# SyncE's queue re-ordered, and the split queries' operand loads of the steps requested by ScalarE

## What is computed

```
x   = x + tanh(g_xattn) * attention(layernorm(x), ctx)        # 16 heads of 32, 120 keys
x   = x + tanh(g_ffn)   * int8_linear(layernorm(x))           # rows quantised to -127..127

attention(x, y):  q = x@Wq + bq ; k = y@Wk + bk ; v = y@Wv + bv
                  weights = softmax(q k^T / sqrt(32)) ; out = (weights v) @ Wo + bo
```

## Time and profile before

| | us |
|---|---|
| median of 3 runs | 819.43 (815.38 to 822.44) |
| profiled execution | 818.51 |
| its span, first to last instruction | 816.4 |

### The profile page before, as it was taken

How to read it: one execution, slowest core, us unless ns; L and a number is a source line. 1 busy time by engine, 2 the same in 40 slices (tenths; PEclk the granted TensorE clock), 3 DMA queues, 4 the chain that set the end, 5 groups by cost and what they waited for, 6 DMA issues and landing times.

```text
span 816.4 us, 16283 instructions
## 1 busy us (share of the span) xinstructions
PE 781.1 (96%) x5890; PEld 533.9 (65%) x5890; DVE 587.0 (72%) x879; ACT 604.4 (74%) x844; POOL 527.9 (65%) x524
## 2 busy tenths in 40 slices
PE   9886889999999999999999999999999999999996
PEld 6654556766677676667666676676766677666563
DVE  5964757787686868867686877868688676766567
ACT  5764557868777786877779687777868777796785
POOL 4826328476684947668494756849476685845587
PEclk9989899999999999999999999999999999999999
DMA  8999796878879688897977889697798868775612
GB/s 307 324 256 222 211 262 180 235 230 247 257 195 269 203 241 250 209 273 197 270 222 219 244 231 270 182 266 218 219 268 240 228 177 246 197 186 169 186 66 103
DMA packets 119518, 183.20 MB, mean 224 GB/s; under 512 B 37648, under 2 KB 47248, under 8 KB 117392
## 3 DMA queue, kind: packets, MB, share of 16 engines
q1 hardware_dynamic: 118720, 181.32, 78.3%
q10 hardware_dynamic: 720, 0.86, 0.3%
HBM read 123.91 MB, written 58.22 MB: 223 GB/s over the span
## 4 chain that ended last, share of the span: by engine, by line
PE 80%; DVE 6%; issue 5%; DMA 4%; POOL 2%; ACT 2%; SPq 1%; DVEq 0%; ACTq 0%; POOLq 0%
PE bank_b L443 26%; PE bank_a L443 16%; PE scores L498 7%; PE sum_ps L525 7%; PE scores L517 7%; PE pv_ps L529 6%; PE bank_a L573 4%; DMA q_rows<-q_parts 3%; DVE row_max L1221 2%; PE bank_b L573 2%; PE scores L443 1%; PE bank_a L548 1%; PE sum_ps L506 1%; PE pv_ps L773 1%; DMA k_rows<-o_lo 1%
## 5 line engine op out<-in xcount | busy, mean ns | idle before, releaser
L1232 DVE TENSOR_TENSOR q_parts<-q_sb,q_parts 128x512 fp32r<-128x512 f32 x60 | 64.0, 1066 | 121.5 <-ACT q_parts L857 121.5
L1577 POOL TENSOR_TENSOR o_lo<-on,o_hi 128x512 fp32r<-128x512 f32 x48 | 64.6, 1346 | 131.8 <-ACT o_hi L906 131.8
L1221 DVE TENSOR_REDUCE row_max<-scores 128x16 f32<-128x1920 f32 x64 | 137.7, 2152 | 10.9 <-PE scores L498 10.8
L888 ACT ACTIVATE probs<-scores 120x2048 f32<-120x2048 f32 x64 | 120.1, 1877 | 27.4 <-PE scores L517 27.3
L1533 POOL TENSOR_TENSOR xt<-xt,rstd_b 128x512 f32<-128x512 f32 x60 | 97.3, 1652 | 3.1 <-ACT rstd_b L1155 1.6
L1585 POOL TENSOR_TENSOR x<-x,gbias_r 128x512 f32<-128x512 f32 x64 | 82.9, 1296 | 23.2 <-ACT cen L912 22.1
L498 PEld LDWEIGHTS scores<-k_sb,q_sb 32*128 32x128 f32 x1984 | 61.0, 186 | 52.0 <-issue 41.1
L1573 POOL TENSOR_TENSOR x<-x,gbo_r 128x512 f32<-128x512 f32 x64 | 93.7, 1476 | 0.1
L906 ACT ACTIVATE o_hi<-on 128x512 fp32r<-128x512 f32 x48 | 30.3, 632 | 84.7 <-DVE on L1245 84.7
L517 PE MATMUL scores<-q_stack,k_stack 128*120 128x512 f32 x256 | 74.0, 411 | 17.3 <-DVE row_max L1221 12.5
L443 PE MATMUL bank_b<-xt_hi,wq_hi 128*128 128x512 f32 x188 | 77.4, 412 | 1.3 <-DVE xt_lo L1211 1.2
(11 more groups left out here) (235 smaller groups left out, 1931.8 us busy)
## 6 DMA issues: line engine op xcount, KB each, us to landing
q_stack<-q_rows SPq DMA_DIRECT2D x192, 256.0 KB, 4.5
q_rows<-q_parts SPq DMA_DIRECT2D x61, 512.0 KB, 4.1
xt<-in_x_t SPq DMA_DIRECT2D x16, 1024.0 KB, 8.1
x<-in_x SPq DMA_DIRECT2D x64, 256.0 KB, 3.3
out_x<-x SPq DMA_DIRECT2D x61, 256.0 KB, 5.0
x_in<-in_x SPq DMA_DIRECT2D x60, 256.0 KB, 5.1
k_stack<-k_rows SPq DMA_DIRECT2D x96, 120.0 KB, 3.9
k_rows<-k_parts SPq DMA_DIRECT2D x28, 240.0 KB, 4.0
```

What stands on the lines that cost most here:

```text
L888: act.activation(probs[0:KEYS], scores[0:KEYS], ACT.Exp, scale=SCALE).then_inc(p_ready, 1)
L1221: dve.tensor_reduce(row_max[:].rearrange("p (t r) j -> p r t j", r=ROWG)[:, :, :, j], scores[:, :, 0:QT * KEYS].rearrange("p r (t k) -> p ...
```

## The change

On SyncE:
- `stack_q` is left only three times, ahead of the steps: groups 0, 1 and 2 of batch 0. `stack_q(0, 0)` moves ahead of `store_q(0, 1)`.
- The five loads of `rest_landed` are spread over the issue order between `store_k(0, 3)` and `load_x(3, 0)`; they and a wait for x_stats stood ahead of `load_ctx(1)`.
- Within a step, `load_x(f, 2)` moves to slot 0 behind `store_q(b, 0)` (in step 0: behind `store_q(1, 1)` in slot 1), and `stack_k(b, 0)` moves behind `store_q(b, 1)` and `load_x(f, 3)`.

On ScalarE: `stack_q` is a function of its own, with the same three DMAs and the same two waits, called behind `split_high(b, j)`. Each slot calls it once (slot 0 of step 0 doesn't): `stack_q(i, 2)`, `stack_q(i, 3)`, `stack_q(b, 0)`, `stack_q(b, 1)` in slots 0 to 3; in `last_step` twice. These are 61 calls, 183 DMAs. In slot 3 `high_x(n, 3)` moves ahead of `copy_max`.

The diff, with the moves inside SyncE's list cut to their result:

```diff
@@ SyncE, ahead of the steps
             load_xt(1)
-            sp.wait_ge(x_stats, nth(0, QT, 3))
-            load(rest_landed, u_sb[:].bitcast(I32), rows(wq8))
-            load(rest_landed, gbo_r[:], bo.partition_broadcast(P))
-            load(rest_landed, gws_r[:], w_scale.partition_broadcast(P))
-            load(rest_landed, gbias_r[:], w_bias.partition_broadcast(P))
-            load(rest_landed, ident_b[:], consts_bf16)
             load_ctx(1)
...
             stack_k(0, 0)
+            stack_q(0, 0)
             store_q(0, 1)
-            stack_q(0, 0)
             store_k(0, 2)
             store_k(0, 3)
+            load(rest_landed, u_sb[:].bitcast(I32), rows(wq8))
             stack_q(0, 1)
...
             load_x(2, 2)
+            load_x(2, 3)
+            load(rest_landed, gbo_r[:], bo.partition_broadcast(P))
             stack_q(0, 2)
-            load_x(2, 3)
             store_q(1, 0)
+            load(rest_landed, gws_r[:], w_scale.partition_broadcast(P))
+            load(rest_landed, gbias_r[:], w_bias.partition_broadcast(P))
+            load(rest_landed, ident_b[:], consts_bf16)
             load_x(3, 0)
@@ SyncE, step(i): slots 0 and 1 (slots 2 and 3 lose stack_q(b, 0), stack_q(b, 1); store_q(b, 2) goes ahead of load_x(f + 1, 0))
-                if i > 0:
-                    stack_q(i, 2)
                 if is_batch(e):
                     store(e, 0)
                 if i > 0 and is_batch(b):
                     store_q(b, 0)
+                if i > 0 and is_batch(f):
+                    load_x(f, 2)
                 if i > 0:
                     load_residual(i, 0)
 
-                stack_q(i, 3)
-                if is_batch(f):
-                    load_x(f, 2)
-                if is_batch(b):
-                    stack_k(b, 0)
                 if is_batch(e):
                     store(e, 1)
                 if is_batch(b):
                     store_q(b, 1)
+                if i == 0:
+                    load_x(f, 2)
                 if is_batch(f):
                     load_x(f, 3)
+                if is_batch(b):
+                    stack_k(b, 0)
@@ ScalarE
+            def stack_q(n, j):
+                act.wait_ge(q_stored[j], stores_of(n, j))
+                act.wait_ge(s_done, nth(n, DT, j) - 2)
+                for block, part in enumerate((0, 1, 0)):
+                    load(q_stacked[j % 2], q_stack[j % 2][STRIPS[block]].bitcast(F32),
+                         q_rows[j, part].rearrange("(r d) s -> d r s", d=DH))
@@ ScalarE, step(i), the four slots, and last_step
                     split_high(b, 0)
+                if i > 0:
+                    stack_q(i, 2)
                 log_sums(i, 0)
...
                     split_high(b, 1)
+                stack_q(i, 3)
                 log_sums(i, 1)
...
                     split_high(b, 2)
+                    stack_q(b, 0)
                 log_sums(i, 2)
...
                     split_high(b, 3)
+                    stack_q(b, 1)
...
                     high_x(n, 2)
+                    high_x(n, 3)
                 if is_batch(b):
                     copy_max(b, sum_ps)
                 high_o(i, 3)
-                if is_batch(n):
-                    high_x(n, 3)
...
                 exponentials(i, 0)
+                stack_q(i, 2)
...
                 exponentials(i, 1)
+                stack_q(i, 3)
```

More of the change, by code:

```diff
@@ L385, in step @@
                     store_q(b, 1)
+                if i == 0:
+                    load_x(f, 2)
                 if is_batch(f):
                     load_x(f, 3)
+                if is_batch(b):
+                    stack_k(b, 0)
                 if i > 0:
                     load_residual(i, 1)
-                if is_batch(b):
-                    stack_q(b, 0)
                 if is_batch(k_of(i)):
@@ L396, in step @@
                     store(e, 2)
+                if is_batch(b):
+                    store_q(b, 2)
                 if is_batch(f + 1):
                     load_x(f + 1, 0)
[L399 to L403, removed]
                 if is_batch(k_of(i)):
```

## The result

| | before | after | ratio (95% interval) |
|---|---|---|---|
| median | 817.4 us, 4 runs (814.67 to 822.44) | 806.68 us, 4 runs (804.38 to 809.15) | 0.9869 (0.9832 to 0.9907) |
| timed once more, beside e7, e8 and e10 (e9) | 818.43 us, 14 runs | 805.93 us, 6 runs (805.03 to 811.2) | 0.986 (0.983 to 0.989) |
| profiled execution, its span | 818.51, 816.4 | 809.15, 807.0 | |

The kernel is 1.3% faster, 10.7 us, and the forecast of 807 is met. Most of the terms that were summed to it are not. To see that, I took the start of every `scores_by_key` (64 of them, L511 now) and subtracted its start in the trace of before; this is the **shift**, and a term of the sum is a change of the shift between two places.

The account below looks back on a forecast made before the run. It took TensorE's own work to bound the middle steps, with gains only in the transfer-filled start. Terms -3.9 - 9.3 + 1.5 - 2.0 + 1.3 = -12.4 from 818.5 gave 806.1, a median of 807 us, range 800 to 824.

Parts of the forecast that it names:

- Part 1: First reload, stack_q(0, 0): lands before TensorE waits at 39.1 us, so attend(0, 0) starts at 45.5, not 49.37: -3.9 us.
- part 2: store_q(1, 1) in step 0: SyncE already waits there when its data comes, so the stall goes: -9.3 us, +1.5 given back.
- part 3: The store at 104.68 in step 1: group 2's reload moves to a second queue, bytes the same: 0.
- part 4: ScalarE issuing 183 DMAs, 1.3 us a slot, mostly in idle time; an earlier exponential in slot 3 saves waits: -2 us.
- first bound of part 2: store_q(1, 1) in step 0: 2.3 MB at 300 GB/s takes 7.7 us, landing at 65.8, so no wait is left.
- The stall of step 1 still there: Sign that the forecast is right: the stall in step 1 remains, some 12 us earlier.
- Stores of q that land over 8 us after issue beside ScalarE's loads: Sign that the forecast is wrong: split-query stores land that late while ScalarE's queue loads.
- taking turns delays the stores: Rival: with two queues, reloads share the engines with stores in steps 0 and 1: +5 to +8, 812 to 815 us; chance 0.11.
- The slower rival: Issuing on ScalarE exceeds its room in slot 3: at 1 us a DMA +25 us, 832; chance 0.14.
- Part 5: SyncE without the reloads: its waits for scores_by_key no longer hold stores behind them; 0 in the middle.
- Part 6: Last step: ScalarE's second 1.3 us of issuing stands ahead of quant_round and z_b, delaying the turn at 774.10: +1.3 us.
- The transfer rival: The start is bound by transfers, so half of parts 1 and 2 is kept: 813 to 815 us; chance 0.17.

Follow-up runs that it names:

- e7: e5 with the keys' first store of step 0 moved ahead of the four put-off loads: 803.24 us, ratio 0.9812 to the kernel before.
- e8: The changed kernel with the first of each slot's three reload DMAs split in two, four issues, same bytes: 809.5 us, ratio 0.9901 to the kernel before.
- e10: e1 plus the edit of e2: SyncE's new order and high_x(n, 3) ahead of copy_max, reloads still on SyncE: 811.66 us, ratio 0.9912 to the kernel before.
- e9: The changed kernel itself, unchanged, run once more: 805.93 us, ratio 0.986 to the kernel before.
- e1: SyncE's new order alone; reloads stay on SyncE at the tops of the slots, high_x(n, 3) where it was: 813.43 us, ratio 0.9956 to the kernel before.
- e2: The kernel before with only high_x(n, 3) moved ahead of copy_max: 815.12 us, ratio 0.9971 to the kernel before.
- e3: The changed kernel with only high_x(n, 3) put back behind high_o: 810.97 us, ratio 0.9919 to the kernel before.
- e4: The changed kernel with the five rest_landed loads and their wait back ahead of load_ctx(1): 806.64 us, ratio 0.9848 to the kernel before.
- e5: The changed kernel with the last four of the five put-off loads moved later, behind load_x(3, 3) in step 0: 808.6 us, ratio 0.9877 to the kernel before.
- e6: The changed kernel with every reload DMA split in two, six issues a slot, same bytes: 837.02 us, ratio 1.0274 to the kernel before.

## Why the prediction was right, and where it was not

The sum was right because its errors cancelled. By its own steps, with the profiled executions of after and of e9:

| step | forecast | after | e9 |
|---|---|---|---|
| 1, first reload | -3.9 | -2.4 | -3.4 |
| 2, store_q(1, 1) | -7.8 | -1.1 | -1.5 |
| 3, the store in step 1 | 0 | -3.4 | -3.6 |
| 4, ScalarE's issues and the copy | -2 | -4.4 | -4.6 |
| 6, last step | +1.3 | 0 | 0 |

(Part 1 is the shift at group 1 of step 0; part 2 what is added by the first scores of step 1; part 3 by step 2; part 4 by group 1 of step 12; the one long instruction of after, +2.46, is in none. Some 0.5 us of part 4 is not the copy's: it is a loss in steps 9 and 10 that stands in the traces of before, e1, e2 and e10, all with the reloads on SyncE's queue, and in none of after, e3, e4, e5, e7, e8 and e9, which have them on ScalarE's. Its cause is open.) The order, parts 1 and 2 together, was forecast at -11.7 us; alone it gave 3.6 us by the medians (e1), and -6.2 by its trace.

**Part 1** had the right mechanism. In e1 and e9 no wait for the reload is left (1.3 and 1.5 us of waiting at that place are put to `copy_max`), TensorE waits 0.73 and 0.74 us for the low part of xt as forecast, and `attend(0, 0)` starts at 45.52 and 45.94. In the trace of after "the reload lands ahead of the 39.1 us" failed: SyncE issued it at 34.68, 1.7 us later than in e9, its three issues took 2.43 us, the last landed at 41.17, and `attend(0, 0)` starts at 46.95. As e9 is the same code, this is a spread between executions that the sum had no term for.

**Part 2 is the step that failed**: "In the new order SyncE is waiting at this store when its data comes". It stood at `load_rstd(2)` until 65.08. I had written that the loads which were put off "cost nothing there", having looked at who needs them and not at what stands behind them on their queue. The waits of the start, kernel by kernel (us; the last column is the shift at group 3 of step 0):

| kernel | rstd stored | read back | data of store_q(1, 1) | issued | landed after | ScalarE waits | shift |
|---|---|---|---|---|---|---|---|
| before | 58.83 | 61.63 | 63.66 | 69.10 | 9.68 | 8.30 | |
| after | 56.29 | 65.08 | 61.20 | 65.98 | 9.16 | 7.14 | -3.58 |
| e9 (after) | 55.28 | 62.59 | 60.22 | 63.68 | 8.51 | 5.15 | -5.75 |
| e8 | 55.46 | 61.14 | 60.47 | 62.07 | 9.31 | 2.58 | -6.47 |
| e4, loads early | 58.77 | 62.55 | 63.70 | 63.73 | 9.27 | 2.48 | -4.88 |
| e7, loads later | 56.60 | 60.70 | 61.30 | 61.60 | 8.59 | 2.09 | -7.65 |
| e5, loads later | 56.02 | 59.48 | 60.97 | 60.99 | 7.93 | 1.15 | -8.87 |

With the loads away from this place the read-back follows the store by 3.5 to 4.1 us (e5, e7, e4); with them there, by 5.7 to 8.8 (after, e9, e8; e1, e3, e6 and e10 lie between). The store then goes out 1.6 to 4.8 us after its data is ready, and at most 0.3 us after it in the other three. So the first bound of part 2 failed as well: the store did not land in 6.0 us (7.7 us of transfers less the head start of xt) in any changed kernel of the table but after 7.9 to 9.3, near the old row's 9.68, and 1.2 to 2.5 us of wait stay even where it goes out at once. Of these three only e5 kept the full clock (1.00 granted from 60 to 100 us). In e4 and e7 it was 0.72 from 76 to 82 us, and from scores to attention they took 5.44 and 5.45 us, after the shorter wait, against 5.68 before. The rest of the spread is in the code of no kernel: after and e9 are one. For the same reason the medians do not show this step by itself (e4 and e5 are level with after); only e7, which mends the next place too, is faster.

**Part 3** was left at 0 with the words "the bytes are the same". The bytes are, their place isn't. Step 1 gained 3.4 and 3.6 us in after and e9 and 2.8 in e3, but also 2.4 in e1 and 0.8 in e10, so a part comes without the second queue; the move of this one reload was not tried alone. Here two signs that the prediction had named must be read. "The stall of step 1 still there" did not come: ScalarE's wait is 0.92 us for 4.80. "Stores of q that land over 8 us after issue beside ScalarE's loads" did: 9.16 us. Yet the rival that this sign stood for, "taking turns delays the stores", is not borne out: on one queue the same store took 12.38, 11.22 and 10.99 us (before, e1, e10), on two 9.16, 9.69 and 10.63 (after, e9, e3), with 54.2% of the DMA engines' time on SyncE's queue and 23.6% on ScalarE's in after. Single traces cross (e2, on one queue, 9.39; e5, on two, 11.50), so what the medians show is only that two queues cost nothing and are worth 3.0 to 4.3 us in sum. The Trainium skill, DMA: Bandwidth & Descriptors, section "Issuing engines are not separate DMA queues", says that a second issuing engine saves only issuing time. The trace agrees at the keys' store, behind 3.87 us of issues. At `store_q(2, 0)` next to no issuing time was saved, and it landed 0.4 to 2.1 us sooner; I take this for the order of the bytes, which the second queue changed, but no run here separates the two.

**Part 4** had the place (slot 3), the mechanism of the gain (the exponential that no longer waits for `high_x`) and the price of an issue there right (about 1.3 us for three). In slot 0 the price was mostly 1.4 to 2.4 us, over the 1.29 that part 4 called "just enough", and still nothing was lost. The issues start 0.06 us after `split_high` has started and run beside its 0.63 us, which the bound of 0.7 had and the sum did not. The size was off: not six waits of 0.51 less something for the room, but 0.53 in each even step and 0.15 in each odd one, since the issues took nothing back. The 0.15 stands at the same place. In step 5 of before `attend` starts 0.48 us after the last matmul of `project_q`, and in e9 0.33:

```profile
291.69 0.40 PE L443 MATMUL bank_b<-xt_hi,wq_lo 128*128 128x512 f32 x1
292.17 1.06 PE L525 MATMUL sum_ps<-probs,ones_f 120*32 120x512 f32 x8
```

```profile
281.91 0.40 PE L437 MATMUL bank_b<-xt_hi,wq_lo 128*128 128x512 f32 x1
282.24 1.06 PE L519 MATMUL sum_ps<-probs,ones_f 120*32 120x512 f32 x8
```

e1 and e3 have the 0.48, e2 the 0.33, so it goes with the copy; it is too short to be listed as a wait. The slower rival's mechanism is e6's; six issues cost 30 us against after by the medians (26 by the profiled executions).

**Part 5** had nothing to show by itself. **Part 6**: in the last step the issues are behind the start of an exponential, and run beside it; ScalarE goes on without a gap. From e9:

```profile
748.94 1.88 ACT L889 ACTIVATE probs<-scores 120x2048 f32<-120x2048 f32 x1 [0.16 <-PE scores L511]
749.00 1.28 ACTq L808 DMA_DIRECT2D q_stack<-q_rows  x3
750.84 1.92 ACT L883 ACTIVATE q_stack<-q_stack 32x2048 fp32r<-32x2048 f32 x1
```

**The transfer rival** (half of the start's gain reappears at the next store) described the start of after better than the forecast did: -7.01 at step 2, where half of the terms is -6.6 and all of them, less what was given back, -11.7. But e7 speaks against a bound of bytes: the same bytes in another order gave 3 us more.

## What to carry to other kernels

A load that nobody needs soon can still have a price where it is put: whatever stands behind it in the queue and is read back at once, here a 2 KB store. When DMAs are re-ordered, follow each small store and its read-back, not only the large ones. A DMA issued beside a long instruction of its engine is nearly free up to that instruction's length and costs idle time beyond it; double the number of issues once to find the edge. And a forecast that is met is no proof of its terms: two parts here that were forecast at 0 and at -2 us made up for one that failed.

## What the runs showed of the hardware

- **One VectorE instruction was held through five of GpSimd's.** The 6.61 us subtraction of after reads two tiles and takes 0.37 to 1.46 us otherwise. It ran from 646.92 to 653.53. GpSimd's timeline in that time has no gap:

```profile
647.00 1.31 POOL L1584 TENSOR_TENSOR o_lo<-on,o_hi 128x512 fp32r<-128x512 f32 x1
648.24 1.30 POOL L1580 TENSOR_TENSOR x<-x,gbo_r 128x512 f32<-128x512 f32 x1
649.48 1.30 POOL L1592 TENSOR_TENSOR x<-x,gbias_r 128x512 f32<-128x512 f32 x1
650.72 1.29 POOL L1580 TENSOR_TENSOR x<-x,gbo_r 128x512 f32<-128x512 f32 x1
651.94 1.32 POOL L1592 TENSOR_TENSOR x<-x,gbias_r 128x512 f32<-128x512 f32 x1
653.35 0.23 POOL L1529 TENSOR_SCALAR ln_var<-ln_mv 128x4 f32<-128x4 f32 x1
```

  It ended when GpSimd's run of large instructions did. The Trainium skill, SBUF — State Buffer, section "SBUF: two separate sides", says that the two engines share a pair of ports which one of them holds "for the whole instruction". If it changed hands after each instruction, VectorE would wait for the one that is running, 1.3 us; here it lost five turns in a row, and TensorE 2.46 us. That the port is what held it is not shown. It came once in after's trace and once in e4's (6.59 us, beside the same five GpSimd instructions; TensorE lost 3.4 us at step 9), and in none of the other ten; why it happens in one execution and not in the next wasn't tried.
- **The time of an issue varies with the place.** Three took ScalarE 1.28 us in most slots and up to 2.4 in others. Six of half the size took 2.7 in most slots, but 4.4 in slot 3 of steps 2 to 5, where three had taken 1.3 as well.
- **The start varies by itself.** The same kernel's shift at step 2 was -7.01 and -8.51, and e1's and e10's, equal up to there but for one copy, -6.16 and -2.37.
